# Flamingo block (mLSTM cross-attention and mixture of experts) on one core: masks in idle rows of a matmul, a polynomial beside a logarithm, and another order of the experts' steps

## The reference

```python
B, S, D, NH, E = 16, 256, 512, 16, 16           # 16 sequences, 16 heads of 32, 16 experts, top 2
q = layernorm(x); k = v = ctx
ig, fg = split([q, k, v] @ [Wi, Wf] + bias)     # gates per head and position
F = cumsum(log_sigmoid(fg))
log_D = where(t <= s, F[s] - F[t] + ig[t], -inf)
D = exp(log_D - max_t(log_D))
C = (qh @ kh.T / sqrt(32)) * D
C = C / (max(|sum_t C|, exp(-max log_D)) + 1e-6)
x = x + tanh(g_xattn) * (head_layernorm(C @ vh) * ln_scale)
# mixture: top-2 of 16 experts by sqrt(softplus(logits)) + bias, capacity 256 rows each
h_e = silu(rows_e @ W1_e.T) * (rows_e @ W3_e.T);  out_e = h_e @ W2_e.T      # inner width 352
x = x + tanh(g_ffn) * (sum_k w_k out_e(k) + shared_expert(layernorm(x)))
```

## Time and profile before

| | us |
|---|---|
| median of 3 runs (lowest, highest) | 823.45 (821.46, 826.2) |
| the profiled execution | 822.99 |
| its span, first to last instruction | 821.2 |
| TensorE busy | 720.1 (88%) |
| VectorE busy | 503.7 (61%) |
| ScalarE busy | 418.2 (51%) |
| GpSimd busy | 387.2 (47%) |
| mean granted clock of TensorE, of full speed | 0.947 |

### The profile page before, as it was taken

One profiled execution on the slowest core, in us unless ns is written; L12 is line 12 of the kernel. 1 busy time (PEld: TensorE's weight loads), 2 busy tenths in 40 slices (PEclk: granted clock), 3 DMA queues, 4 the chain that ended last, 5 costly groups with the idle time before them and its releaser, 6 DMA issues.

```text
span 821.2 us, 20216 instructions
## 1 busy us (share of the span) xinstructions
PE 720.1 (88%) x7408; PEld 607.1 (74%) x7408; DVE 503.7 (61%) x992; ACT 418.2 (51%) x849; POOL 387.2 (47%) x587
## 2 busy tenths in 40 slices
PE   0874089999999998299999999999999999999993
PEld 0542057677767766178889999899999999999992
DVE  4772726667676766786525979443465767676740
ACT  0765336666666665443436323222456666666651
POOL 3111145778777776332211254214236575757553
PEclk9998559999999999599999999999999999999997
DMA  7882183545353530448772321332468888888854
GB/s 257 275 276 88 45 248 109 145 132 163 117 174 109 171 105 3 156 154 306 247 249 102 103 98 57 93 101 68 160 229 213 259 217 256 218 254 220 253 122 51
DMA packets 90720, 135.57 MB, mean 165 GB/s; under 512 B 16720, under 2 KB 44112, under 8 KB 90672
## 3 DMA queue, kind: packets, MB, share of 16 engines
q1 hardware_dynamic: 74128, 107.41, 39.8%
q0 software_dynamic: 7168, 17.04, 10.4%
q10 hardware_dynamic: 9376, 10.49, 3.9%
HBM read 92.32 MB, written 34.21 MB: 154 GB/s over the span
## 4 chain that ended last, share of the span: by engine, by line
PE 52%; DVE 3%; DMA 2%; POOL 1%; ACT 1%; issue 0%; SPq 0%; POOLq 0%; ACTq 0%
PE psH L1184 31%; PE psY L1201 15%; PE psT L1164 2%; PE psR L1225 2%; DMA xT<-over13l 1%; PE psT L1233 1%; DVE xnorm L1591 1%; DMA out<-ystage,sidx 1%; DVE xl L1414 1%; DVE stats L1482 1%; POOL out L1680 1%; PE psG L1240 1%; DVE over13h L1591 1%; ACT over13l L1362 0%; DVE over2l L1582 0%
## 5 line engine op out<-in xcount | busy, mean ns | idle before, releaser
L1184 PE MATMUL psH<-xh,w13h 128*128 128x256 f32 (+1 forms) x768 | 222.7, 290 | 3.0 <-DVE w13l L1426 3.0
L1184 PE MATMUL psH<-xh,w13l 128*128 128x256 f32 (+1 forms) x768 | 216.6, 282 | 0.0
L1184 PE MATMUL psH<-xl,w13h 128*128 128x256 f32 (+1 forms) x768 | 216.0, 281 | 0.0
L1648 POOL TENSOR_TENSOR hl<-sg,hh 128x256 fp32r<-128x256 f32 (+1 forms) x96 | 78.5, 823 | 212.8 <-ACT hh L1299 212.3
L1184 PEld LDWEIGHTS psH<-xh,w13h 128*128 128x128 f32 (+1 forms) x768 | 138.6, 180 | 12.2 <-issue 7.6
L1184 PEld LDWEIGHTS psH<-xl,w13h 128*128 128x128 f32 (+1 forms) x768 | 138.9, 181 | 0.7
L1184 PEld LDWEIGHTS psH<-xh,w13l 128*128 128x128 f32 (+1 forms) x768 | 138.8, 181 | 0.0
L1294 ACT ACTIVATE sg<-psH 128x256 f32<-128x256 f32 (+1 forms) x96 | 36.4, 379 | 132.4 <-PE psH L1184 131.5
L1420 DVE TENSOR_TENSOR sg<-sg,psH 128x256 f32<-128x256 f32 (+1 forms) x96 | 40.0, 417 | 99.7 <-ACT sg L1294 99.7
L709 ACT ACTIVATE dec<-ring 128x512 f32<-128x512 f32 x128 | 76.2, 595 | 44.9 <-PE ring L614 41.8
L785 DVE SCALAR_TENSOR_TENSOR dec<-psQ,dec 128x512 f32<-128x512 f32 x128 | 79.7, 682 | 11.9 <-PE psQ L626 10.1
(11 more groups left out here) (221 smaller groups left out, 1417.1 us busy)
## 6 DMA issues: line engine op xcount, KB each, us to landing
raw<-w13T SPq DMA_DIRECT2D x64, 352.0 KB, 4.3
gcT<-ctxT ACTq DMA_DIRECT2D x8, 1024.0 KB, 5.8
kT<-ctxT SPq DMA_DIRECT2D x16, 512.0 KB, 5.4
qst<-qT_all SPq DMA_DIRECT2D x16, 512.0 KB, 6.3
ctxs<-ctx SPq DMA_DIRECT2D x16, 512.0 KB, 3.5
xn<-xnorm SPq DMA_DIRECT2D x16, 512.0 KB, 3.7
out<-xres SPq DMA_DIRECT2D x16, 512.0 KB, 4.9
raw<-w2T SPq DMA_DIRECT2D x16, 512.0 KB
```

What stands on the lines that cost most here:

```text
L1184: last = nc.tensor.matmul(psH[m][0:n, v, :], w[wp][:, c, col:col + n], x[xp][:, c, :], start=(c == 0 and k == 0), stop=(c == DC - 1 and k ...
L1648: nc.gpsimd.tensor_tensor(hs[u.p][1][0:n, m, :], sg[0:n, m, :], hs[u.p][0][0:n, m, :].bitcast(F32), ALU.subtract).then_inc(hl_ready, 1)
```

## The change

In the **gates** the polynomial starts when the exponential is there and waits for the logarithm only before its last operation; ScalarE loads the table that has both functions before them. GpSimd no longer fills `aml` and `amr` with ones, but builds for each one a mask of 128 rows, spreads it over the 16 heads, and SP copies each to a second buffer.

In the **attention** the masks take the place of the mask product: `aml` and `amr` have 128 rows now, 6 with the decays as before and 122 that add -1e30 above the diagonal within the same matmuls. The last corner, six columns of the last rows, isn't covered by them; VectorE clears it in `dec` with a predicated copy (`clear`), behind a tiny product, and TensorE's values wait for that (`cleared`). The queries of the first two batches are written to `qst` directly, and their loads fall away.

In the **experts' steps** (`soon`, from the second expert on) the results of the preceding expert stand behind the first third. ScalarE's `stage` moves behind `high(u, 0)`, GpSimd's two `give` to its slot 2. In the last step the second weights are split earlier as well. The wait for the low parts of `hs` is split in three.

```diff
@@ log1p_exp, gate_stage
-            dve.wait_ge(e_ready, 2)
-            log1p_exp(nc, c, e[:, :, :], lu[:, :, :], poly[:, :, :], mask[:, :, :])
+            dve.wait_ge(e_ready, 1)
+            log1p_exp(nc, c, e[:, :, :], lu[:, :, :], poly[:, :, :], mask[:, :, :], (e_ready, 2))
...
+            nc.scalar.preload_act_table_set("natural_log_exp_and_others")
...
-            nc.gpsimd.memset(g.aml[:, :, :], 1.0)
-            nc.gpsimd.memset(g.amr[:, :, :], 1.0)
+            c = Chain(pool, pool_chain)
+            for rows, outs, steps in ((maskl, g.aml, ((ALU.not_equal, MASKED, -5, 1, [[-1, P]], 0),
+                                                      (ALU.is_ge, MASKED, P - 2, -1, [[0, P - SPARE - 1]], SPARE + 1))),
+                                      (maskr, g.amr, ((ALU.is_gt, 1.0, 6, -1, [[1, P]], 0),))):
+                c.link(nc.gpsimd.memset(rows[:, :], 0.0))
+                for compare, fill, base, sign, pattern, lo in steps + ((ALU.is_ge, 1.0, -6, 1, [[0, P]], 0),):
+                    c.link(nc.gpsimd.affine_select(out=rows[:, lo:P], in_=rows[:, lo:P], compare_op=compare, fill=fill,
+                                                   base=base, pattern=pattern, channel_multiplier=sign))
+                nc.gpsimd.tensor_copy(outs[0][:, :, :], rows[:, :].rearrange("p (o t) -> p o t", o=1).broadcast_to(
+                    [P, NH, P])).then_inc(masks_ready, 1)
...
+            for k, rows in enumerate((g.aml, g.amr)):
+                sp.wait_ge(masks_ready, k + 1)
+                sp.dma_start(rows[1][:, :, :], rows[0][:, :, :]).then_inc(masks_kept, 16)
@@ attention_stage
+                if b < 2:
+                    sp.sem_inc(q_in[u], 16)
...
-                    nc.tensor.matmul(out[:, gg * P:(gg + 1) * P], aml[32 * c:32 * c + 6, h, :], amr[32 * c:32 * c + 6, h, :],
-                                     start=(gg == 0), stop=(gg == 3), skip_group_check=True)
-                nc.tensor.matmul(out[:, :], g.identb[:, :], g.causal[:, :, :].rearrange("p a t -> p (a t)"), start=False,
-                                 stop=True, skip_group_check=True).then_inc(filled, 1)
+                    last = nc.tensor.matmul(out[:, gg * P:(gg + 1) * P], aml[c][:, h, :], amr[c][:, h, :], start=True, stop=True)
+                last.then_inc(filled, 1)
...
+                pe.wait_ge(cleared, 4 * i + r + 1)
...
+            def clear(i, r):
+
+                c, lo = r % 2, P - 32
+                dve.wait_ge(c_done, 16 * i + 4 * r + 4)
+                nc.vector.tensor_tensor(g.none[:, 0:1], g.none[:, 1:2], g.none[:, 2:3], ALU.mult)
+                wide = lambda t: t[lo:P, :].rearrange("p (o t) -> p o t", o=1).broadcast_to([32, NH, P - SPARE])
+                nc.vector.copy_predicated(dec[c][lo:P, :, :, SPARE:P].rearrange("p k g t -> p (k g) t"),
+                                          wide(g.corner).bitcast(U32), wide(g.zeros)).then_inc(cleared, 1)
@@ mixture_stage, TensorE
-                    pe.wait_ge(hl_ready, 3 * u.q + 3)
...
+                    if j == 0:
+                        pe.wait_ge(hl_ready, 3 * u.q + k + 1)
...
-            def step(before, u, after):
+            def step(before, u, after, soon=False):
                 for m in range(FC):
...
+                    if m == 0 and soon:
+                        for j in range(2):
+                            back(before, j)
                 for j in range(2):
-                    if before:
+                    if before and not soon:
                         back(before, j)
@@ mixture_stage, ScalarE
                 high(u, 0)
+                if soon:
+                    if not after:
+                        split2(u)
+                    for j in range(2):
+                        stage(before, j)
...
-                if before and new_set(before, u):
+                if before and new_set(before, u) and after:
                     split2(u)
@@ mixture_stage, GpSimd
+                    if s == 2 and soon:
+                        give(k - 1, 0)
+                        give(k - 1, 1)
```

More of the change, by code:

```diff
@@ L484, in attention_stage @@
         kT = [a.sb(f"kT{u}", [P, DC, S]) for u in range(2)]
-        qst = [a.sb(f"qst{u}", [P, DC, S]) for u in range(2)]
+        qst = g.qst
         ctxs = [a.sb(f"ctxs{u}", [P, 2, D]) for u in range(2)]
@@ L1342, in step @@
                 high(u, 2)
-                if before and new_set(before, u):
+                if before and new_set(before, u) and after:
                     split2(u)
                 yield
-                if before and not before.shared:
+                if before and not before.shared and not soon:
                     for j in range(2):
@@ L1457, in step @@
                 yield
+                if before and new_set(before, u) and not after:
+                    split2(u)
                 yield
@@ L1683, in give, with step @@
                     compute_op=ALU.add).then_inc(y_out[j], 16)
-            def step(u):
+            def step(before, u, after, soon=False):
+                k = u.q - B
                 for s in range(SLOTS):
@@ L1734, in _ @@
             for q in range(B):
-                for s, _ in enumerate(step(early(q))):
+                for s, _ in enumerate(step(None, early(q), None)):
                     side.issue(SLOTS * q + s, 1)
```

73 lines of the change are left out of this document (41 added, 32 removed).

## The result

| | us |
|---|---|
| kernel before, median of 4 runs | 824.4 |
| changed kernel, median of 4 runs (lowest, highest) | 848.65 (844.77, 850.5) |
| ratio, 95% interval | 1.0292 (1.0243 to 1.0341) |
| the profiled execution of the changed kernel | 847.93 |

The change makes the kernel 2.9% slower. The time is 4.7 us over the forecast of 844 and inside its range.

The account below looks back on a forecast made before the run. TensorE was taken to bound the experts' steps, ScalarE's emptying of banks the attention without masks. Sum: 822.99 - 0.3 - 4.5 - 20.3 + 39.2 + 9 - 2.3 = 844 us; range 828 to 862.

Parts of the forecast that it names:

- The experts' steps, +39.2: Experts' steps: next weights' splits stay behind the later second third, so steps take 16.35 us against 13.58, fourteen times.
- The second wait, of 0.3 us: Experts' steps: results, now 3.29 us into the next step, wait about 0.3 us for the second weights' last part.
- The clock, +9 in half of the steps: Experts' steps: the new 2.5 us pause brings 1.2 GHz in half of them, 1.25 us each, +9 (0 to 17).
- Rival A: Experts' steps: as forecast, but the clock holds at 2.4 GHz through the waits; 835 us, chance 0.22.
- The attention's tiles, -20.3: Attention at full clock: without the mask product each pair of tiles saves 1.40 us, over 14.5 pairs.
- Rival C: Attention: ScalarE's emptying doesn't bind, TensorE saves its whole 2.56 us per pair; 818 us with clock held, chance 0.08.
- Rival E: Attention: more TensorE pauses keep some tiles longer at 1.2 GHz, up to 3 us more each; 850 to 865, chance 0.06.
- Start of the attention, -4.5: Attention's first tiles: earlier first scores and no masks bring the third scores 4.5 us sooner (3 to 6).
- Gates, -0.3: Gates: earlier polynomial gains at best 2.0 us, GpSimd's mask spreading may eat it; 0.3 gained, between -2 and +2.
- Tail, -2.3: Last step to last write: expert 14's additions have long landed, so the write ends 2.3 us sooner (-4 to 0).
- B: Experts' steps: GpSimd's remainders still fall into the low parts, 4.82 us instead of 3.30; 865 us, chance 0.10.
- D: Experts' steps stay at 13.58 us because the weights' split doesn't hang on the second third; 796 us, chance 0.06.

## Why the prediction was right, and where not

**The experts' steps, +39.2: right, by the mechanism named.** The forecast put the low parts at 3.30 us because GpSimd's remainder would be done before them, and so it was (676.53, 3.30). Without the six falls of the clock the fourteen steps cost 47.0 - 5.7 = 41.3 us. The step was to be 16.35 us, and the short ones are 16.57. The difference is small: the results start 3.64 us into the step (680.12 to 683.76) where the sum had 3.6, and 0.29 us lie between the last low part (679.83) and the product, where it had 0.1. The wait of 2.5 us in front of the next expert measured 2.40 and 2.45. Moving the splits made it vanish, as it must if they cause it. The second wait, of 0.3 us, is there in the short steps: 0.68 us pass from the transposes to the results (683.08 to 683.76), in a long step 0.35 (666.83 to 667.18).

**The clock, +9 in half of the steps: right in kind, too large.** It falls in every second pause from the fourth step on, six times at 0.95 us (forecast: seven at 1.25), 5.7 us; the filled pause gave back 5.8. A slow first third costs 1.28 us (4.40 against 3.12), and 0.33 come back because the second wait falls away behind it. That it would be half of them was a guess between two rows, and luck; the regular alternation was not foreseen. Rival A, the clock held through the waits, fell with it. What A describes is the kernel with the filled pause: 840 us, where A had 835 with a larger gain in the attention.

**The attention's tiles, -20.3: mis-sized.** The step that failed is the saving of 1.40 us per pair; over 14.5 pairs it measured 15.1 us, 1.04 each. The even tile came out as forecast (6.37, measured 6.40), the odd one was 5.48 and came out at 5.92 and 5.82. The forecast took the odd tile's exponential, state and exponential for a chain that nothing lengthens, and charged nothing for a product of 128 rows since the mask product had them as well. The rows of the odd tile show where the chain grew. Up to the exponential 0.20 us are saved (1.74 to 1.54) where a saved mask product is worth 0.32: the decay now follows the scores by 1.10 us (211.37 to 212.47) and not by 1.00. And from the exponential to the state there are 0.27 us more (0.51 to 0.78), because the gather waits 0.30 us for VectorE. The two make the 0.39 that are missing in this tile. Of the 0.27 the kernel with the queries scaled later gives back 0.16 (0.78 to 0.62): GpSimd's scaling holds VectorE. The corner is worth 0.06 a pair by itself. The agreement of the even tile is in part luck: with 6 rows it takes 6.18 to 6.24, so the charge that was left out was made up by some saving that was forecast too small; which one is open. Rival C, the full 2.56 us, fell as the wait for the exponential said it would. Rival E fell too: from 117 to 310 us the clock was 1.00.

**Start of the attention, -4.5: nearly right**, 5.8 in the profiled execution. (The terms written out for the third scores add up to 119.8, not 119.6, hence to 4.3.) The saving varies, since TensorE runs at 1.2 GHz there for a time that differs from run to run: from the first scores to the third are 11.7 us in this kernel and 10.4 in the one with the splits moved.

**Gates, -0.3: right in direction and cause**, 0.7 measured. The gain is 1.9 us without the masks, and their spreading takes 1.3 of it back.

**Tail, -2.3: mis-sized**, 1.4 measured. (The forecast's own times, 24.5 and 21.9 us, differ by 2.6.) The forecast placed the last second weights by the engines that split them. Their load is issued at 820.02 and takes 4.96 us, and ScalarE's high parts wait 3.97 us for it. The transfer had no term in the sum. The end of the chain in order of time:

```profile
820.02 4.96 DMA raw<-w2T
...
828.11 1.56 POOL out L1722
...
830.07 5.31 DMA out<-ystage,sidx
...
838.11 1.56 POOL out L1722
```

**Rivals B and D fell.** B needed low parts of 4.82 us; they were 3.30. In the kernel with the splits moved they do take 4.17, but outside the chain. D, steps of 13.58, is what that kernel reaches, at 795.65 us, where D had 796: the new order costs nothing once the splits hang on the right third. That the sums meet so closely is luck, since D counts 20.3 us for tiles that measured 15.1.

Between the forecast of 844.0 and the execution of 847.9 us lie 3.9: +5.2 for the tiles, +1.6 for the slower start of the program, +0.9 for the tail, -1.3 for the attention's start, -1.2 for the steps with the clock, -0.4 for the gates and -0.7 between attention and experts come to 4.1, and the forecast's sum, 843.8, was rounded up by 0.2.

## What to carry to other kernels

When a block of work is moved in an order written out by hand, list what else was placed by the block's old position: here the splits of the next weights hung on the second third, and the move of 4.14 us of results turned into a pause in each of fourteen steps. Look for the second wait behind the first one before trying a cure, since taking away one of two chained waits gave only 28 of 50 us. And test a slow change part by part: two of its three parts gained 2.6%, and the third, finished, gained another 0.5%, of which the last step alone gives 0.3%.

## What the runs showed of the hardware that was not expected

- With 6 rows of weights in the decays' products, and no mask product, the granted clock averaged 0.53 to 0.57 in stretches of the attention loop, with pauses no longer than at full clock. With 128 rows, zeros in 122 of them, it was 1.00 there. The same numbers were computed; the times were 812.29 and 797.93 us.
- A pause of 2.40 to 2.45 us on TensorE was followed by a lower clock every second time, strictly in turn, eleven steps long. 36 small products in the pause (2.18 us) kept the clock at 1.00. Why it alternates was not tried.
- A product with 128 rows of weights follows the scores of 32 rows by 1.10 us, one with 6 rows by 1.00.
- VectorE's product of one column took 0.16 us by itself and up to 1.24 us beside a GpSimd instruction (in the changed kernel both end at 113.5 us), which shows how long one engine is held more clearly than a large operation does.
